# A layernorm taken along the free axis, with its transposition on the vector and scalar engines, and four shifts of order in a fused graph kernel

## What is computed

```python
h = relu(adj @ x @ gcn_w + gcn_b)
h = (h - h.mean(-1)) * rsqrt(h.var(-1) + 1e-5) * ln_g + ln_b
# mamba(h):
xc, z = split(h @ w_in)
u = silu(causal_conv4(xc) + conv_b)
dbc = u @ w_xp;  B, C = dbc[:, 8:24], dbc[:, 24:40]
dt = softplus(dbc[:, :8] @ w_dt + b_dt)
hst = exp(dt * A) * hst + dt * B * u        # scan over nodes, 16 states
y = (sum_s hst * C + u * D_skip) * silu(z)
x1 = layernorm(x + y @ w_out)
# layer 2: two three-layer MLPs, on adj @ x1 and on adj @ x2
out = layernorm(x1 + concat(mlp1(adj @ x1), mlp2(adj @ x2)) @ Wm.T + bm)
```

## Time and profile before

| | |
|---|---|
| median of 3 | 820.49 us (820.03 to 822.79) |
| the profiled execution | 821.7 us, span 819.9 us |
| PE busy | 805.8 us, 98% |
| POOL busy | 659.7 us, 80% |
| DVE busy | 599.7 us, 73% |
| ACT busy | 377.9 us, 46% |
| granted TensorE clock, mean | 0.998 |

### The profile page before, as it was taken

How to read it: one execution, slowest core, us unless ns; L and a number is a source line. 1 busy time by engine, 2 the same in 40 slices (tenths; PEclk the granted TensorE clock), 3 DMA queues, 4 the chain that set the end, 5 groups by cost and what they waited for, 6 DMA issues and landing times.

```text
span 819.9 us, 7302 instructions
## 1 busy us (share of the span) xinstructions
PE 805.8 (98%) x2078; PEld 365.8 (45%) x2078; DVE 599.7 (73%) x800; ACT 377.9 (46%) x615; POOL 659.7 (80%) x318
## 2 busy tenths in 40 slices
PE   8899999999999999999999999999999999999996
PEld 3344444444444444444444444444444454444453
DVE  0034898799868986898799879887988889882135
ACT  0154465357535653475347534652466445231234
POOL 2005999999999899899999999889998999970036
PEclk9999999999999999999999999999999999999999
DMA  8979767675766899899778976789867896887602
GB/s 336 385 270 368 267 242 250 231 251 201 271 202 201 333 349 355 343 352 361 245 249 320 379 278 213 254 291 384 295 235 272 327 329 245 297 306 261 254 26 78
DMA packets 63388, 227.59 MB, mean 278 GB/s; under 512 B 7394, under 2 KB 8052, under 8 KB 44916
## 3 DMA queue, kind: packets, MB, share of 16 engines
q1 hardware_dynamic: 24660, 156.33, 50.9%
q10 hardware_dynamic: 38688, 70.80, 26.4%
HBM read 224.48 MB, written 2.62 MB: 277 GB/s over the span
## 4 chain that ended last, share of the span: by engine, by line
PE 95%; DMA 4%; ACT 1%; DVE 0%; issue 0%; DVEq 0%
PE p_x L486 51%; PE p_x L509 16%; PE p_two L509 11%; DMA x_s<-x_tiles 3%; PE p_m L582 2%; PE p_dA L677 2%; PE p_m L598 2%; PE p_two L572 1%; PE p_m L565 1%; DMA ring<-adj_blocks 1%; PE p_m L602 1%; PE p_m L536 1%; PE p_m L542 1%; PE p_h L677 1%; PE p_m L594 1%; PE p_two L552 1%
## 5 line engine op out<-in xcount | busy, mean ns | idle before, releaser
L486 PE MATMUL p_x<-ring,x_s 128*128 128x512 f32 x1024 | 459.2, 597 | 4.2 <-DMA x_s<-x_tiles 4.2
L1125 POOL TENSOR_TENSOR y<-y,prod 128x1024 f32<-128x1024 f32 x127 | 299.4, 2357 | 26.6 <-DVE prod L942 25.9
L486 PEld LDWEIGHTS p_x<-ring,x_s 128*128 128x128 f32 x1024 | 193.8, 191 | 252.1 <-issue 242.5
L1116 POOL TENSOR_TENSOR bh<-spread,dtu 128x1024 f32<-128x1024 f32 x128 | 302.1, 2360 | 2.1 <-DMA spread<-bc_rows 2.0
L933 DVE TENSOR_TENSOR_SCAN p_h<-p_dA,state,bh 128x512 f32<-128x512 f32 x224 | 276.2, 1279 | 25.3 <-ACT p_dA L687 11.3
L687 ACT ACTIVATE p_dA<-dt,A 128x512 f32<-128x512 f32 x256 | 170.8, 686 | 113.0 <-DVE p_h L933 109.9
L942 DVE TENSOR_TENSOR prod<-p_h,spread_C 128x1024 f32<-128x1024 f32 x128 | 155.3, 1213 | 0.0
L509 PE MATMUL p_x<-ring,x 128*128 128x512 f32 x304 | 137.2, 593 | 0.0
L509 PE MATMUL p_two<-ring,x 128*128 128x512 f32 x208 | 94.5, 593 | 0.5 <-DVE dt L992 0.5
L509 PEld LDWEIGHTS p_x<-ring,x 128*128 128x128 f32 x304 | 57.4, 190 | 72.6 <-issue 72.6
L415 POOL TENSOR_SCALAR dtu<-prod,mv,rstd 128x128 f32<-128x128 f32 x26 | 20.3, 794 | 64.0 <-ACT rstd L920 64.0
(11 more groups left out here) (125 smaller groups left out, 579.9 us busy)
## 6 DMA issues: line engine op xcount, KB each, us to landing
ring<-adj_blocks SPq DMA_DIRECT2D x143, 1024.0 KB, 7.2
spread<-bc_rows ACTq DMA_DIRECT2D x128, 256.0 KB, 5.1
spread_C<-bc_rows ACTq DMA_DIRECT2D x128, 256.0 KB, 5.7
ring<-adj_blocks SPq DMA_DIRECT2D x8, 256.0 KB, 5.8
x_s<-x_tiles SPq DMA_DIRECT2D x8, 256.0 KB, 7.4
x_s<-x_tiles ACTq DMA_DIRECT2D x7, 256.0 KB, 7.5
out_tiles<-dtu SPq DMA_DIRECT2D x7, 256.0 KB, 2.0
pack<-pack_w ACTq DMA_DIRECT2D x1, 1026.5 KB, 11.2
```

Source lines behind the costliest of these rows:

```text
L486: return pe.matmul(bank[:, :], tiles[:, JT * m + jt, :], ring[:, i % RING, jt, :], start=opens, stop=closes)
L1116: pool.tensor_tensor(bh[:, i % 3, :, :], both(spread[:, i % SLOTS, :]), dtu[:, c % 2, :, :], ALU.mult).then_inc(s_bmul, 1)
L1125: pool.tensor_tensor(y[:, c % 2, :, :], y[:, c % 2, :, :], prod[:, i % 2, :, :], ALU.add).then_inc(s_acc, 1)
```

## The change

- **Layernorm of the first layer.** `gcn` becomes four matmuls of 128x128 with the roles exchanged (`ax` is stationary, gcn_w moves), so nodes lie on partitions and the mean is along the free axis. It moves to half 6. DVE (`stats`, unit 3, place 0) does relu with the bias in two instructions, four bn_stats and four bn_aggr. ACT (`norm`, unit 3): Ln, Exp, a negation, four shifts, four normalisations of 128x128. DVE (`turn`, unit 4): one transposition of 128x512 in 32x32 blocks. ACT (`moves`, unit 4): 16 copies of 32 partitions x 4x32 put the blocks in place; in chunk 0 eight of them go to DVE. The matmuls `cen` and `var`, the matrices `cen_w` and `mean_w` and the fold matmul are gone; ln_g goes onto w_in by one DVE instruction.
- **dt.** `dt_sum` writes into its PSUM banks; ACT copies them out (`dt_copy`, unit 11); `dtu` is two DVE products (unit 11, place 1) from the banks, in place of POOL's one. PE's `z`, `mlp0` and the first use of `p_two` after unit 4 wait for `dtu` where they waited for `dt_sum`.
- **Order.** The first softplus stands ahead of the two first broadcasts. `x_s` is asked for one block sooner and `pack` comes behind all of it. `out` moves to half 3 (DVE, ACT: unit 2), the MLP to halves 25 to 31 (the last one to 22 to 28), and after the last chunk one block, not two, stands ahead of `out`. `nmean` on DVE is replaced by a negation of rstd on ACT, and the last chunk copies no state.

The core of the diff (semaphore names and shapes of constants left out):

```diff
-FILL = {"gcn": 0, "cen": 1, "var": 3, "in_x": 7, "x_proj": 3, "dt": 18}
+FILL = {"gcn": 12, "in_x": 7, "x_proj": 3, "dt": 10}
...
-        return [(c - 1, (24, 26, 28, 30))]
-    return [(6, (6, 9, 12, 15)), (7, (24, 26, 28, 30))]
+        return [(c - 1, (25, 27, 29, 31))]
+    return [(6, (6, 9, 12, 15)), (7, (22, 24, 26, 28))]
...
-        put(2, 0, "out", c - 1)
+        put(1, 1, "out", c - 1)
...
-        at = tuple(2 * origin(c) + q - (c == 0) for q in (-1, 1, 2, 4, 9, 12))
-        for name, q in zip(("gcn", "cen", "var", "in_x", "x_proj", "dt"), at):
+        at = tuple(2 * origin(c) + q for q in (-2, 4, 9, 12))
+        for name, q in zip(("gcn", "in_x", "x_proj", "dt"), at):
...
                         if unit > origin(chunk) and chunk + 1 < NC:
-                            pe.wait_ge(s_dt, G * (chunk + 1) + 1)
+                            pe.wait_ge(s_dtu, G * (chunk + 1) + 1)
...
-                    pe.matmul(p_m[:, :], gcn_w, ax[:, n % 2, :], start=True, stop=True).then_inc(s_gcn, 1)
-                elif name == "cen":
-                    pe.wait_ge(s_hr, n + 1)
-                    pe.matmul(p_m[:, :], cen_w[:, :], hr[:, :], start=True, stop=True).then_inc(s_cen, 1)
-                elif name == "var":
-                    pe.wait_ge(s_sq, n + 1)
-                    pe.matmul(p_m[:, :], mean_w[:, :], sq[:, :], start=True, stop=True).then_inc(s_var, 1)
+
+                    for t in range(JT):
+                        last = pe.matmul(p_m4[:, t, :], ax[:, n % 2, P * t:P * (t + 1)], gcn_w, start=True, stop=True)
+                    last.then_inc(s_gcn, 1)
...
             block_part(AFTER_AT, 0, JT)
-            block_part(AFTER_AT + 1, 0, JT)
             step("out", NC - 1)
...
+                if name == "norm":
+
+                    act.wait_ge(s_hst, 2 * n + 2)
+                    act.activation(rstd[:, 2 + b, :], mv[:, 2 + b, :, 1], ACT.Ln, bias=eps_t[:, :]).then_inc(s_hrs, 1)
...
+                elif name == "moves":
+
+                    act.wait_ge(s_turn, n + 1)
                     wait(act, s_z, G * n)
...
+                    for q in range(P // Q if n else MOVES_0):
+                        for r in range(P // Q):
+                            last = act.activation(hr4[Q * r:Q * (r + 1), :, Q * q:Q * (q + 1)],
+                                                  turned[Q * q:Q * (q + 1), :, Q * r:Q * (r + 1)], ACT.Copy)
+                    last.then_inc(s_h, 1)
...
+                elif name == "dt_copy":
+                    for q, (g, bank) in enumerate(((1, p_two), (0, p_m))):
+                        act.wait_ge(s_dtsum, G * n + q + 1)
+                        act.activation(dt_[:, b, g, :], bank[:, :], ACT.Copy).then_inc(s_dt, 1)
...
-                if name == "rows":
+                if name == "softplus":
                     for i in range(AHEAD):
                         spread_row(i)
...
+                if name == "stats":
+                    dve.wait_ge(s_gcn, n + 1)
+
+                    dve.scalar_tensor_tensor(out=p_m4, in0=gb_tiles, scalar=-1.0, in1=p_m4,
+                                             op0=ALU.mult, op1=ALU.max).then_inc(s_gb, 1)
+                    dve.wait_ge(s_gb, n + 1)
+                    dve.tensor_tensor(sq4, p_m4, gb_tiles, ALU.add).then_inc(s_relu, 1)
...
+                elif name == "turn":
+                    dve.wait_ge(s_norm, n + 1)
+                    wait(dve, s_h, n)
+                    dve.transpose(turned[:, :, :].rearrange("p t n -> p (t n)"), sq[:, :]).then_inc(s_turn, 1)
...
+                elif name == "dtu":
+
+                    dve.wait_ge(s_u, G * (n + 1))
+                    for q, (g, bank) in enumerate(((1, p_two), (0, p_m))):
+                        dve.wait_ge(s_dt, G * n + q + 1)
+                        dve.tensor_tensor(dtu[:, b, g, :], bank[:, :], u[:, g, :], ALU.mult).then_inc(s_dtu, 1)
```

More of the change, by code:

```diff
@@ L15 @@
 G = 2
+Q = 32
 S = 16
@@ L29 @@
 STAGES = 4
+MOVES_0 = 2
 WARM, WARM_W = 2, 256
@@ L620, in _ @@
             pe.wait_ge(s_pack, 16)
+            for q in range(2 * G):
+                last = pe.matmul(p_h[:, 1, q:q + 1], w_in[:, P * q:P * (q + 1)], w("ln_b"), start=True, stop=True)
+            last.then_inc(s_bxzp, 1)
             pe.wait_ge(s_wx3, 1)
-            pe.wait_ge(s_mean_w, 1)
             pe.wait_ge(s_wdt, 32)
             tile = 0
-            for name in ("gcn", "cen", "var", "in_x", "x_proj", "dt"):
+            for name in ("gcn", "in_x", "x_proj", "dt"):
                 step(name, 0)
-                if name == "gcn":
-                    for q in range(2 * G):
-                        last = pe.matmul(p_h[:, 1, q:q + 1], w_in[:, P * q:P * (q + 1)], w("ln_b"),
-                                         start=True, stop=True)
-                    last.then_inc(s_bxzp, 1)
-                    pe.wait_ge(s_cen_w, 1)
-                    pe.wait_ge(s_gw, 1)
-                    pe.matmul(p_h[:, 0, :], cen_w[:, :], u[:, 0, :], start=True, stop=True).then_inc(s_wp, 1)
                 for _ in range(FILL.get(name, 0)):
@@ L649, in _ @@
             block_part(AFTER_AT, 0, JT)
-            block_part(AFTER_AT + 1, 0, JT)
             step("out", NC - 1)
-            for i in range(AFTER_AT + 2, TAIL_AT):
+            for i in range(AFTER_AT + 1, TAIL_AT):
                 block_part(i, 0, JT)
@@ L835, in steps_of @@
                     o = origin(c)
-                    put(o - 1, "gcn", c + 1)
-                    put(o, "cen", c + 1)
-                    put(o + 1, "var", c + 1)
+                    put(o - 1, "norm", c + 1)
+                    put(o, "moves", c + 1)
                     put(o + 2, "in_x", c + 1)
@@ L865, in _ @@
             take_x(0)
-            for name in ("gcn", "cen", "var", "in_x", "silu", "log_exp", "x_part", "rows", "softplus", "y_init"):
+            for name in ("norm", "moves", "in_x", "silu", "log_exp", "x_part", "rows", "softplus", "dt_copy", "y_init"):
                 step(name, 0)
-                if name == "gcn":
-                    act.wait_ge(s_wp, 1)
-                    act.activation(w_in, p_h[:, 0, :], ACT.Copy).then_inc(s_win, 1)
+                if name == "norm":
                     act.wait_ge(s_scales, 1)
-                if name == "rows":
+                if name == "softplus":
                     for i in range(AHEAD):
@@ L1027, in steps_of @@
                     o = origin(c)
-                    put(o + 2, 0, "var", c + 1)
+                    put(o - 1, 0, "stats", c + 1)
+                    put(o, 0, "turn", c + 1)
                     put(o + 3, 0, "taps0", c + 1)
@@ L1032, in steps_of @@
                     put(o + 7, 0, "dt_sum", c + 1)
+                    put(o + 7, 1, "dtu", c + 1)
                 return table
@@ L1051, in _ @@
             dve.wait_ge(s_two_add, 1)
-            for name in ("var", "taps0", "taps1", "x_sum", "dt_sum"):
+            for name in ("stats", "turn", "moves", "taps0", "taps1", "x_sum", "dt_sum", "dtu"):
                 step(name, 0)
@@ L1076, in _ @@
             add_sum(SUM_OF[AFTER_AT])
-            add_sum(SUM_OF[AFTER_AT + 1])
             step("out", NC - 1)
-            for no in range(SUM_OF[AFTER_AT + 2], SUM_OF[TAIL_AT]):
+            for no in range(SUM_OF[AFTER_AT + 1], SUM_OF[TAIL_AT]):
                 add_sum(no)
@@ L1163, in _ @@
             pool.tensor_copy(wx3[:, :, ROW_B + S:ROW_B + 2 * S], w_xp[:, :, R + S:R + 2 * S]).then_inc(s_wx3, 1)
-            step("dtu", 0)
             for i in range(AHEAD):
@@ L1174, in _ @@
                         step("gate_y", c - 1)
-                    if c + 1 < NC and unit == origin(c) + 8:
-                        step("dtu", c + 1)
                     if i + AHEAD < S * NC:
```

150 lines of the change are left out of this document (82 added, 68 removed).

## The result

| | before | after |
|---|---|---|
| median | 820.49 us (819.10 to 823.83, 5 runs) | 816.49 us (815.58 to 818.27, 5 runs) |
| profiled execution, span | 819.9 us | 816.5 us |
| PE busy | 805.8 us | 794.2 us |
| POOL busy | 659.7 us | 641.5 us |
| granted TensorE clock, mean | 0.998 | 0.992 |

The ratio is 0.9951, 95% interval 0.9933 to 0.9969. The time lies in the range that was given, but near its upper end, where the rival "DVE late by a little" was put (813 to 818), and the gain is under half of the forecast's.

What follows compares the result with a forecast made beforehand. PE, busy 98% of the span, was taken to set the time. -2.3 up to A, -6.8 from A to B and -0.9 to the end made -10.0, so 810.5 us from the median 820.49; range 804.5 to 818.5.

Steps and rivals of the forecast that it cites:

- DVE late by a little: Second rival: margin 0.7 at `x_proj` fails in three 12-step chunks, chunk 2's wait is 6; 813 to 818, chance 0.15.
- PE's list: Matmul work leaving PE: 1.69 us a chunk, 13.5 for eight, and 0.86 for the fold, 14.4 us.
- The start: Both waits for `x_s` go, row 0 ends at 36.2 instead of 39.03; 3.2 us is waited away by A.
- A: Start of `x_proj` in chunk 1, 114.82 before; forecast 112.5 (109.3 to 114.5), so -2.3 us.
- Chunk 1: PE done with `gcn` at 163.6, DVE there about 165.5: a wait of 1.4 us (0 to 3).
- Chunk 2: The sum in `p_two` now waits for `dtu`: 4.1 us (4 to 6, if DVE is late).
- The 7.75: Chunk 2, `dt` start to `dtu`: 4.45 to `dt_sum`, 1.25 its parts, 1.3 product with C, 0.7 `dtu`.
- The bound of 6: Upper bound in us of chunk 2's wait for `dtu`, if DVE is late.
- thinnest margin: At `x_proj` in chunks 1, 3 and 4: `u` after 25.7 us, PE needs 26.4, margin 0.7.
- Chunks 4 to 7 and the end: No later wait at `in_x`; after B one adjacency step fewer, -0.9 us; 3 to 4 us left at last `out`.
- B: Start of `x_proj` in chunk 7, 622.17 before; forecast 613, with -6.8 us from A to B.
- 12-step chunks: Chunks 1, 3 and 4, where 12 adjacency steps stand between `in_x` and `x_proj`; margin 0.7 us.

Runs made afterwards that it cites:

- x_behind: The changed kernel with the start's loads in the old order (packed weights behind x tile 6, old gates for x): 814.37 us, ratio 0.9926.
- chunk2_order: The changed kernel with chunk 2's list reordered, all of row 5's x blocks ahead of the x1 blocks of rows 2 and 3: 809.96 us, ratio 0.9876.
- out_mlp_undone: The changed kernel with the output product, its sum and x1 one place later and the mlp steps one half sooner, as before: 816.66 us, ratio 0.9948.
- chunk2_order_b: As chunk2_order, but with row 6's first x block between the two pairs of x1 blocks: 809.76 us, ratio 0.9852.
- softplus_behind: The changed kernel with chunk 0's first two broadcasts issued ahead of softplus again: 817.76 us, ratio 0.9964.
- dt_undone: The changed kernel with the dt part alone put back: sum to `dt_`, no ScalarE copies, `dtu` product on GpSimd: 811.31 us, ratio 0.9870.
- copies_twice: The changed kernel with ScalarE's 16 copies of the transposed blocks made twice for chunks 1 to 7: 850.77 us, ratio 1.036.
- dtu_early: The changed kernel with `dtu` one place sooner on VectorE, ahead of the product with C: 814.99 us, ratio 0.9912.

## Why the forecast was wrong, point by point

**PE's list** was right: `cen` and `var` are gone from it, no chunk waits at `in_x`, and PE's busy time is 11.6 us less although some 4 us of it are lost to slow steps (14.4 were to leave the list).

**The start** was right in its sum: row 0 ends at 36.6 (forecast 36.2). Of the two waits for `x_s` that were to go, the second did; one of 1.3 us is left near 15.8. That what is won there is waited away by A was right in part: of the 2.3 us that x_behind gives up at `dt` of chunk 0, 1.2 are still there at `x_proj`.

**A** is 113.39, forecast 112.5: +0.9. The copies took 5.1 us, 0.32 apart, where 0.21 apart and 3.4 were taken (bounds 0.11, the author's estimate, which no row shows, and 0.60). The 0.30 for one was right (0.307); that the next starts before the last has ended, as two exponentials on 128 partitions do (0.69 us each, 1.30 for both), did not hold for these copies. They held the exp of unit 6, and the scan behind waited 1.6 us for it. From the start of `stats` (87.29) to the end of the last copy (100.00) are 12.7 us; the forecast wrote 11.5, but its terms add up to 11.05, and 11.05 with the 1.7 of the longer copies is what was measured. The 0.9 itself is less than A moves from one execution to another: in chunk2_order, out_mlp_undone and chunk2_order_b, with the same code up to there, it is at 112.04, 111.97 and 113.70. The transposition was 0.69 us (0.65 taken; the upper bound of 1.3 was the author's estimate, which no row shows).

**Chunk 1** had 1.4 us forecast, as a wait for DVE at `gcn`, and 1.7 were found, but of another kind: a lower clock behind the wait at `x_proj`. PE doesn't wait at that `gcn`. The size came out right by luck.

**Chunk 2 is the step that failed.** Forecast: `dtu` 7.75 us after `dt` starts, a wait of 4.1. Measured: 9.9 us (284.54 to 294.48), a wait of 6.2. The 7.75 had a product with C of 1.3 us that starts at once; it started 1.9 late, for a broadcast that took 11.5 us while the DMA engines were full. Where that transfer came in time (x_behind, softplus_behind) the wait was 4.2 and 4.3 us, so the other terms of the 7.75 were right. The bound of 6, "if DVE is late", would nearly have held it. What had no term at all is what a wait of this length does to the steps behind it: 2.2 us. The third miss is apart from this wait: `x_proj` in chunk 3 waited 1.2 us, where none was taken, and it waits 1.0 and 1.2 in chunk2_order and chunk2_order_b too, where nothing waits for `dtu`, but not in x_behind and out_mlp_undone, where PE had waited 4.2 and 6.3 for it. The forecast had its thinnest margin there, 0.7 us; which of its terms was short is not shown. Together the three are 9.6 us in place of 4.1. Both reorderings, and dt_undone by another way, take away the wait (or most of it) and the slow steps, and the time falls by 5 to 7 us each time (6 to 8 by the ratios).

**Chunks 4 to 7 and the end** were right: no wait at `in_x` or `x_proj` there, and from B to the end 196.9 us, forecast 196.8. The margin at the last `out` held.

Added up on the spans: forecast -10.0, measured -3.4. Of the 6.6 us between, 0.9 were lost at A, 0.3 in chunk 1, and 5.4 in chunks 2 and 3: 4.3 of them at the wait for `dtu` and in the slow steps behind it, the rest at the next `x_proj`.

The rival that came true is the second, in its part on chunk 2; its other part, 12-step chunks that each wait, did so in chunk 3 alone.

## What to carry to other kernels

Price a wait on the bottleneck engine twice: its length, and what the clock may take from the work behind it (here from nothing to 3.0 us: in softplus_behind the eight steps behind the wait of 4.3 us took 9.86 from start to start, 293.68 to 303.54). When a wait is moved from one result to a later one, follow what stands ahead of that result in its engine's list, down to the transfers, and take the slow end of their landing times, not the median. And if a new dependency bites at a single place of the schedule, move the work there: eight steps in another order gave more here, 6 to 8 us by the ratios, than the whole change had.

## What was not expected of the hardware

- A wait of 6.2 us on PE was followed by a stretch at a granted clock of 0.61, one of 3.6 us by 0.72, costing 2.2 and 1.8 us over eight steps; one of 1.8 us in the same place left it at 1.00. Between these lengths the clock did either: it fell behind three of six waits of 1.9 us at `x_proj` and behind one of 2.7 us in copies_twice, and stayed behind three waits of 3.1 to 3.3 us in the same run.
- A broadcast of one row to 128 partitions (256 KB written) reached DVE after 11.5 us with the DMA engines full, against a median of 5.6. In the same place it took 11.1 and 11.6 us in dtu_early and out_mlp_undone, 6.5 and 7.2 in softplus_behind and x_behind.
- ScalarE copies of 32 partitions x 128 elements took 0.307 us each, 0.32 apart, so they don't overlap, where two 128x512 exponentials of 0.69 us took 1.30 together. Eight copies of the same shape on DVE took 0.218 us each, 0.23 apart.
